# Attention and mixture-of-experts layer: a new order of work between the two stages, one PSUM place per tile for the last expert, and the variance's constant moved to VectorE

## The chip, the cores and the metric

One core of a Trainium2 chip. The metric is the device time of one execution in microseconds; lower is better. The kernel before takes 196.55 us (median of 3 runs, 196.53 to 196.87).

## The reference

The input is a tensor of 8 batches, 256 tokens each, 128 features. Two steps follow each other:

```
qkv = x @ w_qkv.T                 # 16 heads of 8 dimensions
att = softmax(mask(q k^T / sqrt(8)))    # keys i-127 .. i only
x   = layernorm(x + (att v) @ w_out.T)
probs = softmax(x @ router_w); top 2 of 8 experts per token, weights from probs
y   = sum over the 2 chosen experts of p * (gelu(x @ w_in[e] + b_in[e]) @ w_out[e] + b_out[e])
out = layernorm(x + y)            # (x - mean) / sqrt(var + 1e-5)
```

The kernel computes every expert for every token and multiplies with a gate that is zero where the expert wasn't chosen.

## The kernel before, in words

It is written engine by engine: each engine has its own list of instructions, in an order fixed by hand, and they meet through semaphores.

**Attention.** The batches 0 to 7 go through a pipeline of slots. A slot holds at most one pair of heads on each engine. For a pair n (8 per batch, 64 in all), PE multiplies keys by queries (`turned_scores`, L1067), ACT takes the exponential of the result into `probs` (L486), and for each two pairs (a quad, 4 per batch) POOL sets the forbidden places to zero with two affine selects (`mask_probs`, L443 and L445), whereupon PE weighs the values (`weigh_values`, L1089 and L1091) into `o_bank`. Up to pair 53 the scores go into the pair of PSUM banks `st`; pairs 54 and later alternate between `st` and `score_banks` 0 and 1, so that `turned_scores` of pair n waits only for exponential n - 2.

A batch is finished by a chain over four engines: ACT copies `o_bank` (`copy_output`, L528), PE transposes it (`turn_output`, L1127), VectorE divides by the sums (`normalise`, L735 and L743), PE transposes (`turn_attention`, L1138), ACT copies (L535), PE multiplies by the output weights (`project_out`, L1145), VectorE adds the residual and takes the statistics (L751, L758, L764), POOL takes variance plus constant to the power -1/2 (`first_deviation`, L435 and L437), VectorE normalises (`first_norm`, L770), PE transposes (`turn_x1`, L1154), ACT copies (L543), VectorE splits the copy into two halves of precision (L777, L779), and PE multiplies by the router's weights (L1161).

**Between the stages.** The slots 65 and later hold no new scores of a batch, only the last eleven pairs and what remains of batches 5, 6 and 7. There PE's slots are filled up with products of zeros that nobody reads (`keep_warm`, L977, two of 128x512 in each of eight slots). In the same slots VectorE splits the experts' first weights (`split_weights`, L784 and L786, 1024 columns each) and chooses the experts of the first four batches (`route_shift`, `choose`: L664 to L694, small operations of 64 columns in a row that depend on each other).

**Experts.** The tokens go in four chunks c of 512, a chunk in four tiles of 128. Per chunk and expert PE multiplies by the first weights in three passes (`first_layer`, L1173), ACT applies gelu (L594), PE multiplies by the second weights, four tiles into the four quarters of one PSUM bank (`second_layer`, L1187), and VectorE adds each tile, times its gate, to the rows (`add_share`, L860). After the last expert of a chunk VectorE takes statistics of the rows (`second_stats` L902, `second_moments` L908); POOL adds the constant (L468) and takes the power (L470), both for half a chunk, two tiles, at a time (`second_deviation`). In the last chunk VectorE normalises (`second_norm`, L915) and SP stores each half (L353).

```
second_layer(c, e):   wait gelu_done;  wait y_added >= (n - 3) * 4;  4 tiles;  y_ready += 1
add_last_expert(c):   wait y_ready;  shares 0, 1, 2;  stats of half 0;  share 3;
                      moments of half 0;  stats of half 1;  moments of half 1
```

Of the kernel before, what the change touches and what calls it, by code (L numbers as in the profile page):

```python
# [7 lines left out]
ALU = mybir.AluOpType  # L8
# [3 lines left out]
P = 128  # L12
B = 8
T = 256
E = 128
H = 16
D = E // H
NX = 8
# [8 lines left out]
QUADS = H // 4  # L27
TILES = B * T // P
CH = 512
CT = CH // P  # L30
NCH = B * T // CH
# [49 lines left out]
def attention_moe(nc, x_t, x, wqkv_t, wout_t, router_w, w_in, b_in_t, w_out, b_out, out):  # L81
    scratch = nc.dram_tensor("scratch", [2, 2, ROWS, 2, PAIRS * T], BF16, kind="Internal").ap()

    with ExitStack() as ctx:  # L84
# [3 lines left out]
        def sem(name):  # L88
            return ctx.enter_context(nc.semaphore(name))
# [7 lines left out]
        hid_bank = [score_bank[2], score_bank[0]]  # L97
        y_bank = [score_bank[1], st[:, 0, :], st[:, 1, :], o_bank[:, :]]
        gate_bank, bias_bank = misc

        ident = sb("ident", [P, P])
        ident_bf = sb("ident_bf", [P, P], BF16)
# [99 lines left out]
        hid_ready, gelu_done, y_ready, y_added = sem("hid_ready"), sem("gelu_done"), sem("y_ready"), sem("y_added")  # L202
        bias_added, stats2_done, moments2_done = sem("bias_added"), sem("stats2_done"), sem("moments2_done")
        eps2_added, rstd2_done, y_normed = sem("eps2_added"), sem("rstd2_done"), sem("y_normed")
        shift2_ready = sem("shift2_ready")
        stored = [sem(f"stored{i}") for i in range(2)]

        def pair_banks(n):
# [151 lines left out]
        def _(pool):  # L360
# [103 lines left out]
            def second_deviation(c):  # L464
                for half in range(2):
                    two = slice(2 * half, 2 * half + 2)
                    pool.wait_ge(moments2_done, c * CT + 2 * half + 2)
                    pool.tensor_scalar(var2[:, two], moments2[:, two, 1], EPS, None, ALU.add).then_inc(eps2_added, 1)  # L468
                    pool.wait_ge(eps2_added, c * 2 + half + 1)
                    pool.tensor_tensor(rstd2[:, two], var2[:, two], half_power[:, two], ALU.pow).then_inc(rstd2_done, 1)  # L470

# [7 lines left out]
        def _(act):  # L479
# [71 lines left out]
            def route_exponentials(tiles, k):  # L551

                act.wait_ge(route_shifted, k)
                nc.scalar.activation(route[1][:, tiles, :], route[0][:, tiles, :], ACT.Exp).then_inc(route_exp, 1)
# [18 lines left out]
            for n in range(PICKED):  # L573
                take_even(n)

            for slot in range(LAST_S2 + 1):
                n = pair_at(slot)
                if n is not None:
                    exponentials(*n)
                for offset, piece in ((TURN_MAX, copy_max), (TURN_ATTN, copy_attention), (PROJECT_QK, take_top), (PROJECT_QK + 1, take_middle),  # L580
                                      (VALUES, pad_v), (COPY_O, copy_output), (TURN_X1, copy_x1), (LOGITS, copy_logits)):
                    b = batch_at(slot, offset)
                    if b is not None:
                        piece(b)
                if slot == LAST_S1 + 3:
                    route_exponentials(EARLY, 1)

            def gelu(c, e):

# [57 lines left out]
        def _(dve):  # L647
# [208 lines left out]
            def token_rows(c, n):  # L856
                return x1[:, c * CT + n, :]

            def add_share(c, e, n):
                nc.vector.scalar_tensor_tensor(token_rows(c, n), y_bank[e % 4][:, n * E:(n + 1) * E], gate[:, c * CT + n, e:e + 1],  # L860
                                               token_rows(c, n), ALU.mult, ALU.add).then_inc(y_added, 1)

            def add_tile(c, e, n):
# [14 lines left out]
            def add_last_expert(c):  # L878

                dve.wait_ge(y_ready, c * NX + NX)  # L880
                for n in range(3):
                    dve.wait_ge(y_added, c * (NX * CT) + (NX - 2) * CT + n + 1)
                    add_share(c, NX - 1, n)
                second_stats(c, 0)
                dve.wait_ge(y_added, c * (NX * CT) + (NX - 1) * CT)
                add_share(c, NX - 1, 3)
                second_moments(c, 0)
                second_stats(c, 1)
                second_moments(c, 1)

            def add_bias(c):

                dve.wait_ge(bias_ready, c + 1)
                dve.wait_ge(y_added, c * (NX * CT) + (NX - 2) * CT)
                rows = x1[:, c * CT:(c + 1) * CT, :]
                nc.vector.tensor_tensor(rows, bias_bank[:, :].rearrange("p (n e) -> p n e", n=CT), rows, ALU.add).then_inc(bias_added, 1)
# [7 lines left out]
            def second_moments(c, half):  # L904

                dve.wait_ge(stats2_done, c * CT + 2 * half + 2)
                for n in (2 * half, 2 * half + 1):
                    nc.vector.bn_aggr(moments2[:, n, :], stats2[:, n, :]).then_inc(moments2_done, 1)  # L908

            def second_norm(c, half):  # L910

# [45 lines left out]
            for c in range(2, NCH):  # L957
                add_expert(c, 0)
                second_shift(c - 1)
                for e in range(1, NX - 2):  # L960
                    add_expert(c, e)
                add_bias(c)
                add_expert(c, NX - 2)
                dve.wait_ge(y_normed, c * CT)
                add_last_expert(c)
            second_norm(NCH - 1, 0)
            second_norm(NCH - 1, 1)

# [2 lines left out]
        def _(pe):  # L971
            mm = nc.tensor.matmul

            def keep_warm(count, bank=o_bank[:, :]):

                for _ in range(count):
                    mm(bank, idle_rows[:, 0:P], idle_rows[:, :], start=True, stop=True)  # L977
# [186 lines left out]
            def first_layer(c, e):  # L1164

                n = c * NX + e
                if n == 1:
                    pe.wait_ge(exp_done, B * PAIRS - 1)
                if n >= 2:
                    pe.wait_ge(gelu_done, n - 1)  # L1170
                cols = slice(c * CH, (c + 1) * CH)
                for i, (w, xx) in enumerate(((w_in_lo, x1_hi), (w_in_hi, x1_lo), (w_in_hi, x1_hi))):
                    last = mm(hid_bank[e % 2], w[:, e, :], xx[:, cols], start=i == 0, stop=i == 2)  # L1173
                last.then_inc(hid_ready, 1)

            def second_layer(c, e):

                n = c * NX + e
                pe.wait_ge(gelu_done, n + 1)
                if n >= 4:  # L1180
                    pe.wait_ge(y_added, (n - 3) * CT)
                if n == 1:
                    pe.wait_ge(exp_done, B * PAIRS)
                if n == 3:
                    pe.wait_ge(o_copied, B)
                for i in range(CT):
                    last = mm(y_bank[e % 4][:, i * E:(i + 1) * E], hid[e % 2][:, i * P:(i + 1) * P], w_out_sb[:, e, :], start=True, stop=True)  # L1187
                last.then_inc(y_ready, 1)

            def turn_gates(c):  # L1190

# [33 lines left out]
                pick_pair(n)  # L1225
            pe.wait_ge(consts_ready, 7)

            for slot in range(LAST_S2 + 1):
                n = pair_at(slot)
                if n is not None:  # L1230
                    turned_scores(*n)
# [45 lines left out]
                b = batch_at(slot, PROJECT_QK + 1)  # L1277
                if b is not None:
                    subtract_top(b)
                if slot > LAST_S1 + 1 and slot < LAST_S2 - 1:  # L1280
                    keep_warm(2, hid_bank[0])
                if slot == LAST_S2 - 1:
                    pe.wait_ge(w_lo_done, 1)
                    first_layer(0, 0)

            weigh_values(B - 1, QUADS - 2)
            first_layer(0, 1)
            second_layer(0, 0)
            weigh_values(B - 1, QUADS - 1)
            unit(0, 2)  # L1290
            turn_x1(B - 2)
            unit(0, 3)
# [71 lines left out]
```

## Time and profile before

| | |
|---|---|
| median of 3 runs | 196.55 us |
| the profiled execution, its own time | 196.5 us |
| its span, first to last instruction | 194.8 us |
| PE busy | 169.4 us (87%) |
| VectorE busy | 154.8 us (79%) |
| ACT busy | 114.6 us (59%) |
| POOL busy | 84.1 us (43%) |
| mean granted TensorE clock | 0.994 |

Times in the profile count from the start of the span; 1.7 us of the execution lie outside it. The attention pipeline with its eleven last pairs ends at about 128 us, the experts of chunk 0 begin there, chunk 3 ends at 188 us, and what follows is VectorE, POOL and the stores.

### The profile page before, as it was taken

To read this page: it belongs to the slowest core of one execution; us is meant where nothing else is said; L and a number is where in the kernel's file an instruction comes from. 1 tells how busy PE (TensorE), PEld (TensorE's weight loads), DVE (VectorE), ACT (ScalarE), POOL (GpSimd) and SP (SyncE) were. 2 spreads that over 40 slices of the span, in tenths; PEclk is the share of its full clock that TensorE was granted. 3 is DMA by queue.
4 is the path that set the end of the run, shared out by engine and by line. 5 is a ranking of instruction groups with operands and counts; after the bars stand their busy time and mean duration, and the time that the engine had idled before them with its cause. 6 is when DMAs were issued, how large, how long until landed. Compare 5 with 4: busy or idle time off the path is not lost. (4 is left out here: it accounts for less than half of the span.)

```text
span 194.8 us, 6184 instructions
## 1 busy us (share of the span) xinstructions
PE 169.4 (87%) x2450; PEld 121.5 (62%) x2460; DVE 154.8 (79%) x468; ACT 114.6 (59%) x216; POOL 84.1 (43%) x157
## 2 busy tenths in 40 slices
PE   7579887988989989889999899989999979999950
PEld 3354454655656656556656544558988869999950
DVE  6985959669598698697988999635798869898793
ACT  4542056687686766876857757564353784564720
POOL 7960006556563655746738366561043002603003
PEclk9999999999999999999999999999999999999997
DMA  5589594194780882955901000000000000020011
GB/s 142 148 232 222 168 242 132 53 212 125 158 226 11 176 206 72 214 160 110 218 13 57 2 8 0 3 0 0 5 0 0 3 27 27 0 59 0 3 53 54
DMA packets 23127, 17.25 MB, mean 89 GB/s; under 512 B 1827, under 2 KB 21179, under 8 KB 23099
## 3 DMA queue, kind: packets, MB, share of 16 engines
q1 hardware_dynamic: 23099, 16.87, 35.2%
q8 instruction: 19, 0.31, 0.7%
q14 instruction: 9, 0.07, 0.1%
HBM read 9.35 MB, written 7.34 MB: 86 GB/s over the span
## 5 line engine op out<-in xcount | busy, mean ns | idle before, releaser
L486 ACT ACTIVATE probs<-st 128x768 f32<-128x768 f32 x59 | 47.9, 811 | 23.8 <-PE st L1067 20.6
L443 POOL TENSOR_SCALAR_AFFINE_SELECT probs<-probs 128x1024 f32<-128x1024 f32 x32 | 35.1, 1097 | 57.4 <-ACT probs L486 57.3
L713 DVE TENSOR_REDUCE max_parts<-score_banks 128x2 f32<-128x384 f32 x64 | 32.6, 550 | 4.6 <-PE score_banks L1041 4.2
L594 ACT ACTIVATE hid<-score_banks,b_in_sb 128x512 f32<-128x512 f32 x32 | 21.9, 687 | 21.0 <-PE score_banks L1173 20.9
L716 DVE TENSOR_REDUCE max_parts<-score_banks 128x4 f32<-128x512 f32 x32 | 20.6, 686 | 13.6 <-PE score_banks L1041 13.6
L1067 PE MATMUL st<-stack 51*64 51x256 bf16 (+1 forms) x472 | 21.2, 254 | 6.2 <-ACT probs L486 5.7
L1030 PE MATMUL score_banks<-edges,ident_bf 64*64 64x256 bf16 (+1 forms) x192 | 19.0, 296 | 4.5 <-DVE max_parts L713 3.4
L1089 PE MATMUL o_bank<-probs,v 128*32 128x256 f32 x256 | 20.4, 391 | 0.0
L445 POOL TENSOR_SCALAR_AFFINE_SELECT probs<-probs 128x512 f32<-128x512 f32 x32 | 20.3, 634 | 0.0
L1067 PEld LDWEIGHTS st<-stack 51*64 51x64 bf16 (+1 forms) x472 | 8.6, 104 | 18.7 <-ACT probs L486 11.8
L860 DVE SCALAR_TENSOR_TENSOR x_rows<-st,gate,x_rows 128x128 f32<-128x128 f32 x64 | 18.1, 344 | 2.4 <-PE st L1187 2.0
L1041 PE MATMUL score_banks<-stack 48*64 48x192 bf16 (+2 forms) x512 | 19.1, 224 | 0.0
L1187 PEld LDWEIGHTS st<-w_out_sb,hid 128*128 128x128 f32 x128 | 16.6, 191 | 2.9 <-ACT hid L594 1.7
L1187 PE MATMUL st<-w_out_sb,hid 128*128 128x128 f32 x128 | 17.0, 276 | 1.3 <-ACT hid L594 1.3
L1173 PE MATMUL score_banks<-x_hi,w_in_lo 128*128 128x512 f32 x32 | 15.4, 480 | 0.0
L1030 PEld LDWEIGHTS score_banks<-edges,ident_bf 64*64 64x64 bf16 x192 | 7.5, 105 | 10.3 <-DVE max_parts L713 4.7
L1041 PEld LDWEIGHTS score_banks<-stack 48*64 48x64 bf16 x512 | 13.9, 107 | 0.0
L1091 PE MATMUL o_bank<-probs,v 128*32 128x128 f32 x256 | 12.9, 273 | 0.0
L1173 PE MATMUL score_banks<-x_hi,w_in_hi 128*128 128x512 f32 x32 | 12.6, 393 | 0.0
L1173 PE MATMUL score_banks<-x_lo,w_in_hi 128*128 128x512 f32 x32 | 12.6, 393 | 0.0
L468 POOL TENSOR_SCALAR var<-moments 128x2 f32<-128x2 f32 x8 | 1.7, 216 | 24.1 <-DVE moments L908 24.1
L1091 PEld LDWEIGHTS o_bank<-probs,v 128*32 128x32 f32 x256 | 8.3, 110 | 5.5
(136 smaller groups left out, 331.2 us busy)
## 6 DMA issues: line engine op xcount, KB each, us to landing
stack<-scratch SPq DMA_DIRECT2D x28, 192.0 KB, 4.0
scratch<-parts SPq DMA_DIRECT2D x16, 192.0 KB, 4.0
scratch<-parts SPq DMA_DIRECT2D x24, 128.0 KB, 3.8
x_rows<-x SPq DMA_DIRECT2D x4, 256.0 KB, 5.6
out<-y_sb SPq DMA_DIRECT2D x8, 128.0 KB, 1.8
x_t_sb<-x_t SPq DMA_DIRECT2D x3, 256.0 KB, 4.8
w_in_sb<-w_in SPq DMA_DIRECT2D x1, 512.0 KB, 5.8
w_out_sb<-w_out SPq DMA_DIRECT2D x1, 512.0 KB, 7.9
```

Of the source, the lines that this page charges most:

```text
L443: pool.affine_select(out=own, in_=own, compare_op=ALU.is_ge, fill=0.0, base=0, pattern=[[0, 2], [0, 4], [1, P]], channel_multiplier=-1).th ...
L486: nc.scalar.activation(probs[g][:, :, two, :].rearrange("p k j c -> p j k c"), pair_banks(PAIRS * b + p)[:, :, 0:3 * P].rearrange("p j (k ...
L594: nc.scalar.activation(hid[e % 2][:, :], hid_bank[e % 2], ACT.Gelu_apprx_tanh, bias=b_in_sb[:, e:e + 1]).then_inc(gelu_done, 1)
L713: nc.vector.tensor_reduce(top[:, 1, r, pair:pair + 2], bank[:, 0:384].rearrange("p (h c) -> p h c", h=2), X_AXIS, ALU.max, negate=True).th ...
L716: nc.vector.tensor_reduce(top[:, 0, r, pair:pair + 4], bank[:, :].rearrange("p (h c) -> p h c", h=4), X_AXIS, ALU.max, negate=True).then_i ...
L1030: mm(at, ident_bf[rows, 64 * r:64 * r + 64], mask, start=True, stop=True)
L1041: last = mm(bank[lo:lo + 64, i * width:i * width + keys.stop - keys.start], q[rows, pair + i, queries], k[rows, pair + i, keys], start=Fal ...
L1067: last = mm(to[cols, r, kt * T:kt * P + T], k[rows, p, at:at + 64], q[rows, p, kt * P:T], start=b > 0 or kt == 0, stop=b > 0, skip_group_c ...
L1089: last = mm(o_bank[rows, t * T:(t + 1) * T], v, probs[g][:, 0:2, j, :], start=s == 0, stop=s == 1, skip_group_check=True)
L1091: last = mm(o_bank[rows, t * T + P:(t + 1) * T], v, probs[g][:, 2, j, :], start=False, stop=s == 1, skip_group_check=True)
L1173: last = mm(hid_bank[e % 2], w[:, e, :], xx[:, cols], start=i == 0, stop=i == 2)
L1187: last = mm(y_bank[e % 4][:, i * E:(i + 1) * E], hid[e % 2][:, i * P:(i + 1) * P], w_out_sb[:, e, :], start=True, stop=True)
```

## The change

Three edits.

- PE and ACT leave the slot loop after slot 64, and what they do from there to the first layer of the first expert is written out in a list of its own. The 16 products of zeros become 2. On PE `weigh_values` comes before `turn_attention` of batch 5, pair 62 of the scores comes after `turn_attention` of batch 6 and not before, and the first layer of expert 0 comes after the last scores. On ACT `copy_output` of batch 6 comes two exponentials earlier, and the copy of batch 6's attention one. VectorE's, POOL's and SP's loops over the slots are as they were.
- In chunk 3 the second layer of expert 7 writes its four tiles into four different banks, with a signal after each; VectorE takes shares 0 and 1, statistics and moments of half 0, then the same for half 1. PE waits there for one more expert's shares (29 * 4 instead of 28 * 4).
- In all four chunks variance plus constant is computed on VectorE behind `bn_aggr`, and POOL is left with the power.

```diff
+        last_banks = [y_bank[(NX - 1) % 4][:, 0:E], gate_bank[:, 0:E], hid_bank[0][:, 0:E], y_bank[(NX - 4) % 4][:, 0:E]]
...
             def second_deviation(c):
                 for half in range(2):
                     two = slice(2 * half, 2 * half + 2)
-                    pool.wait_ge(moments2_done, c * CT + 2 * half + 2)
-                    pool.tensor_scalar(var2[:, two], moments2[:, two, 1], EPS, None, ALU.add).then_inc(eps2_added, 1)
                     pool.wait_ge(eps2_added, c * 2 + half + 1)
                     pool.tensor_tensor(rstd2[:, two], var2[:, two], half_power[:, two], ALU.pow).then_inc(rstd2_done, 1)
...
-            for slot in range(LAST_S2 + 1):
+            for slot in range(LAST_S1 + 1):
...
+            late, last = B - 2, B - 1
+            exponentials(late, 5)
+            copy_max(last)
+            exponentials(late, 6)
+            copy_attention(late - 1)
+            exponentials(late, 7)
+            route_exponentials(EARLY, 1)
+            exponentials(last, 0)
+            exponentials(last, 1)
+            pad_v(last)
+            copy_output(late)
+            exponentials(last, 2)
+            exponentials(last, 3)
+            copy_x1(late - 1)
+            exponentials(last, 4)
+            copy_logits(late - 1)
+            exponentials(last, 5)
+            copy_attention(late)
+            exponentials(last, 6)
+            exponentials(last, 7)
...
+            def finish_last_expert(c):
+
+                for half in range(2):
+                    for n in (2 * half, 2 * half + 1):
+                        dve.wait_ge(last_tiles, n + 1)
+                        dve.wait_ge(y_added, c * (NX * CT) + (NX - 2) * CT + n + 1)
+                        add_share(c, NX - 1, n)
+                    second_stats(c, half)
+                    second_moments(c, half)
...
                 for n in (2 * half, 2 * half + 1):
                     nc.vector.bn_aggr(moments2[:, n, :], stats2[:, n, :]).then_inc(moments2_done, 1)
+                two = slice(2 * half, 2 * half + 2)
+                dve.wait_ge(moments2_done, c * CT + 2 * half + 2)
+                if c:
+                    dve.wait_ge(rstd2_done, (c - 1) * 2 + half + 1)
+                nc.vector.tensor_scalar(var2[:, two], moments2[:, two, 1], EPS, None, ALU.add).then_inc(eps2_added, 1)
...
                 if n >= 4:
-                    pe.wait_ge(y_added, (n - 3) * CT)
+                    pe.wait_ge(y_added, (n - 3 + (n == NCH * NX - 1)) * CT)
...
-                if slot > LAST_S1 + 1 and slot < LAST_S2 - 1:
-                    keep_warm(2, hid_bank[0])
-                if slot == LAST_S2 - 1:
-                    pe.wait_ge(w_lo_done, 1)
-                    first_layer(0, 0)
-
-            weigh_values(B - 1, QUADS - 2)
+
+            late, last = B - 2, B - 1
+            turned_scores(late, 5)
+            turn_max(last)
+            turned_scores(late, 6)
+            weigh_values(late, 1)
+            turn_attention(late - 1)
+            turned_scores(late, 7)
+            weigh_values(late, 2)
+            project_out(late - 1)
+            keep_warm(2, hid_bank[0])
+            turned_scores(last, 0)
+            turned_scores(last, 1)
+            project_v(last)
+            weigh_values(late, 3)
+            turned_scores(last, 2)
+            turned_scores(last, 3)
+            turn_x1(late - 1)
+            turn_output(late)
+            turned_scores(last, 4)
+            route_logits(late - 1)
+            weigh_values(last, 0)
+            turned_scores(last, 5)
+            turn_attention(late)
+            turned_scores(last, 6)
+            weigh_values(last, 1)
+            project_out(late)
+            turned_scores(last, 7)
+            weigh_values(last, 2)
+            pe.wait_ge(w_lo_done, 1)
+            first_layer(0, 0)
             first_layer(0, 1)
             second_layer(0, 0)
-            weigh_values(B - 1, QUADS - 1)
+            weigh_values(last, 3)
```

PE at the start of the stretch between the stages, before: pair 54 of the scores (L1067), `turn_attention` of batch 5 (L1138), `weigh_values` (L1089, L1091), products of zeros (L977), pair 55, `project_out` (L1145).

```order
L1067 MATMUL score_banks<-stack 64x256 x4
L1067 MATMUL score_banks<-stack 64x128 x4
L1138 MATMUL misc<-ident,attn 128x128 x2
L1089 MATMUL o_bank<-probs,v 32x256 x4
L1091 MATMUL o_bank<-probs,v 32x128 x4
L977 MATMUL score_banks<-idle_rows 128x512 x2
L1067 MATMUL st<-stack 64x256 x4
L1067 MATMUL st<-stack 64x128 x4
L1145 MATMUL misc<-wout_sb,attn_t 128x128 x2
```

The same place in the changed kernel, whose line numbers are 38 higher here.

```order
L1105 MATMUL score_banks<-stack 64x256 x4
L1105 MATMUL score_banks<-stack 64x128 x4
L1127 MATMUL o_bank<-probs,v 32x256 x4
L1129 MATMUL o_bank<-probs,v 32x128 x4
L1176 MATMUL misc<-ident,attn 128x128 x2
L1105 MATMUL st<-stack 64x256 x4
L1105 MATMUL st<-stack 64x128 x4
L1127 MATMUL o_bank<-probs,v 32x256 x4
L1129 MATMUL o_bank<-probs,v 32x128 x4
L1183 MATMUL misc<-wout_sb,attn_t 128x128 x2
```

`weigh_values` has moved ahead of the transposition, and pair 55 follows that directly, with neither `weigh_values` nor products of zeros between them.

VectorE at the end of the program, before: the shares of expert 7 (L860), statistics (L902), moments (L908), normalisation (L915).

```order
L860 SCALAR_TENSOR_TENSOR x_rows<-o_bank,gate,x_rows 128x128 x3
L902 BN_STATS stats<-x_rows 128x6 x2
L860 SCALAR_TENSOR_TENSOR x_rows<-o_bank,gate,x_rows 128x128
L908 BN_AGGR moments<-stats 128x2 x2
L902 BN_STATS stats<-x_rows 128x6 x2
L908 BN_AGGR moments<-stats 128x2 x2
L915 TENSOR_SCALAR y_sb<-x_rows,moments,rstd 128x128 x4
```

The same place in the changed kernel (L943 is variance plus constant).

```order
L880 SCALAR_TENSOR_TENSOR x_rows<-o_bank,gate,x_rows 128x128
L880 SCALAR_TENSOR_TENSOR x_rows<-misc,gate,x_rows 128x128
L932 BN_STATS stats<-x_rows 128x6 x2
L938 BN_AGGR moments<-stats 128x2 x2
L943 TENSOR_SCALAR var<-moments 128x2
L880 SCALAR_TENSOR_TENSOR x_rows<-score_banks,gate,x_rows 128x128 x2
L932 BN_STATS stats<-x_rows 128x6 x2
L938 BN_AGGR moments<-stats 128x2 x2
L943 TENSOR_SCALAR var<-moments 128x2
L950 TENSOR_SCALAR y_sb<-x_rows,moments,rstd 128x128 x4
```

Every operation of half 0 now directly follows the one that it needs, and two operations are added.

## Rows read from the trace of the kernel before

**Rows 1.** Busy us by stretch: PE, PE's weight loads, VectorE, ACT, POOL; then granted clock.
```profile
112.00:125.00 13.00, 12.10 (x161) 6.14 (x164) 12.14 (x34) 8.11 (x18) 7.66 (x10) 1.00 0.01 3
157.40:187.80 30.40, 30.40 (x223) 27.99 (x223) 25.78 (x103) 17.77 (x32) 5.94 (x16) 1.00 0.08 23
```
**Rows 2.** The chain of waits, in order of time: start us, us, what.
```profile
187.91 1.03 DVE x_rows L860 x4
...
189.83 0.22 POOL var L468
...
191.07 0.75 POOLq L84
```
**Rows 3.** Timeline of VectorE between the stages: start us, us, operation, [idle before].
```profile
114.20 1.22 DVE L786 TENSOR_TENSOR w_in_lo<-w_in_sb,w_in_hi 128x1024 fp32r<-128x1024 f32 x1
...
117.48 0.23 DVE L675 TENSOR_TENSOR route<-route,row_stat 128x64 f32<-128x64 f32 x1
...
118.26 1.07 DVE L678 TENSOR_TENSOR route<-route,row_stat 128x64 f32<-128x64 f32 x1
...
121.37 0.93 DVE L678 TENSOR_TENSOR route<-route,row_stat 128x64 f32<-128x64 f32 x1
...
124.25 0.62 DVE L743 TENSOR_TENSOR attn<-misc,inv_sum 128x64 f32<-128x64 f32 x4
128.14 0.43 DVE L751 TENSOR_TENSOR resid<-misc,x_rows 128x256 f32<-128x256 f32 x1 [3.27 <-PE misc L1145]
```
**Rows 4.** Timeline of POOL between the stages.
```profile
115.18 1.20 POOL L443 TENSOR_SCALAR_AFFINE_SELECT probs<-probs 128x1024 f32<-128x1024 f32 x1 [1.56 <-ACT probs L486]
...
117.23 0.70 POOL L437 TENSOR_TENSOR rstd<-var_eps,half_power 128x2 f32<-128x2 f32 x1
118.16 1.09 POOL L443 TENSOR_SCALAR_AFFINE_SELECT probs<-probs 128x1024 f32<-128x1024 f32 x1 [0.23 <-ACT probs L486]
```
**Rows 5.** Timeline of PE between the stages.
```profile
112.20 0.44 PE L1138 MATMUL misc<-ident,attn 128*128 128x128 f32 x2 [0.68 <-ACT max_t L508]
...
115.54 0.64 PE L1089 MATMUL o_bank<-probs,v 128*32 128x256 f32 x8
...
116.33 0.60 PE L977 MATMUL score_banks<-idle_rows 128*128 128x512 bf16 x2
...
120.23 0.44 PE L1154 MATMUL misc<-ident,x_rows 128*128 128x128 f32 x2
...
125.05 0.44 PE L1138 MATMUL misc<-ident,attn 128*128 128x128 f32 x2
...
130.38 1.16 PE L1187 MATMUL score_banks<-w_out_sb,hid 128*128 128x128 f32 x8 [0.60 <-ACT hid L594]
```
**Rows 6.** Timeline of ACT: exponential 55, the last of batch 6.
```profile
114.30 0.81 ACT L486 ACTIVATE probs<-st 128x768 f32<-128x768 f32 x1 [1.18 <-PE st L1067]
```
**Rows 7.** Timeline of VectorE at the end.
```profile
187.04 1.13 DVE L860 SCALAR_TENSOR_TENSOR x_rows<-st,gate,x_rows 128x128 f32<-128x128 f32 x4
188.09 0.86 DVE L860 SCALAR_TENSOR_TENSOR x_rows<-o_bank,gate,x_rows 128x128 f32<-128x128 f32 x3
188.86 0.48 DVE L902 BATCH_NORM_STATS2 stats<-x_rows 128x6 f32<-128x128 f32 x2
...
189.50 0.24 DVE L908 BATCH_NORM_AGGREGATE moments<-stats 128x2 f32<-128x6 f32 x2
189.66 0.46 DVE L902 BATCH_NORM_STATS2 stats<-x_rows 128x6 f32<-128x128 f32 x2
190.15 0.25 DVE L908 BATCH_NORM_AGGREGATE moments<-stats 128x2 f32<-128x6 f32 x2
```
**Rows 8.** Timeline of VectorE behind chunk 0: the smallest operation, and its wait.
```profile
150.36 0.16 DVE L921 SCALAR_TENSOR_TENSOR shift<-moments,rstd 128x4 f32<-128x4 f32 x1 [0.47 <-POOL rstd L470]
```
**Rows 9.** The two stretches behind PE's last product; third number from the right: granted clock.
```profile
187.90:192.40 4.50, 0.00 (x0) 0.00 (x0) 3.62 (x18) 0.00 (x0) 1.81 (x4) 1.00 0.10 30
192.40:194.80 2.40, 0.00 (x0) 0.00 (x0) 0.05 (x1) 0.00 (x0) 0.00 (x0) 0.51 0.37 108
```

More of the change, by code:

```diff
@@ L204, in attention_moe @@
         eps2_added, rstd2_done, y_normed = sem("eps2_added"), sem("rstd2_done"), sem("y_normed")
-        shift2_ready = sem("shift2_ready")
+        shift2_ready, last_tiles = sem("shift2_ready"), sem("last_tiles")
         stored = [sem(f"stored{i}") for i in range(2)]
@@ L584, in _ @@
                         piece(b)
-                if slot == LAST_S1 + 3:
-                    route_exponentials(EARLY, 1)
+            late, last = B - 2, B - 1
[18 more added lines that the diff above has]
+            exponentials(last, 7)
             def gelu(c, e):
@@ L859, in add_share @@
             def add_share(c, e, n):
-                nc.vector.scalar_tensor_tensor(token_rows(c, n), y_bank[e % 4][:, n * E:(n + 1) * E], gate[:, c * CT + n, e:e + 1],
+                y = last_banks[n] if c * NX + e == NCH * NX - 1 else y_bank[e % 4][:, n * E:(n + 1) * E]
+                nc.vector.scalar_tensor_tensor(token_rows(c, n), y, gate[:, c * CT + n, e:e + 1],
                                                token_rows(c, n), ALU.mult, ALU.add).then_inc(y_added, 1)
@@ L964, in _ @@
                 dve.wait_ge(y_normed, c * CT)
-                add_last_expert(c)
+                if c < NCH - 1:
+                    add_last_expert(c)
+                else:
+                    finish_last_expert(c)
             second_norm(NCH - 1, 0)
@@ L1186, in second_layer @@
                 for i in range(CT):
-                    last = mm(y_bank[e % 4][:, i * E:(i + 1) * E], hid[e % 2][:, i * P:(i + 1) * P], w_out_sb[:, e, :], start=True, stop=True)
-                last.then_inc(y_ready, 1)
+                    at = y_bank[e % 4][:, i * E:(i + 1) * E]
+                    if n == NCH * NX - 1:
+                        at = last_banks[i]
+                    last = mm(at, hid[e % 2][:, i * P:(i + 1) * P], w_out_sb[:, e, :], start=True, stop=True)
+                    if n == NCH * NX - 1:
+                        last.then_inc(last_tiles, 1)
+                if n < NCH * NX - 1:
+                    last.then_inc(y_ready, 1)
             def turn_gates(c):
@@ L1226, in _ @@
             pe.wait_ge(consts_ready, 7)
-            for slot in range(LAST_S2 + 1):
+            for slot in range(LAST_S1 + 1):
                 n = pair_at(slot)
```

## The prediction

> **What bounds the kernel now.** I read the busy times by stretch first, then the chain of waits, then the timelines of the engines at the two places that the change touches.
>
> From 157.4 to 187.8 us PE is busy without a gap, 30.40 of 30.40 us [rows 1]. Its work there is untouched, so whatever time PE loses or wins before it arrives at the end undiminished. Between the stages, from 112 to 125 us, two engines are nearly full: PE with 12.10 us, part of which is products of zeros, and VectorE with 12.14 us, all of it needed [rows 1]. The difference matters. The filler on PE can only be won if nobody else sets the pace. The timeline says who does: `normalise` of batch 6 starts at 124.25 and ends at 124.87 [rows 3], and PE transposes its result at 125.05, 0.18 us later [rows 5]. VectorE has no such partner: it waits for PE only behind that, 3.27 us at 128.14 [rows 3]. So between the stages **VectorE is the bound**, and PE's filler stands in time that PE would otherwise wait.
>
> At the end the chain is VectorE's shares (from 187.91), then POOL's four operations, the last of them done at 191.82 [rows 2]. PE isn't in it: its last product ends at 187.9, while VectorE takes up expert 7 at 188.09 directly behind expert 6, four shares at a distance of 0.26 us from 187.04 [rows 7].
>
> **Part 1: the new order between the stages.** It removes 14 products of zeros. Two of them take 0.60 us [rows 5], so some 4 us of PE, at nothing or at a gain of nothing as long as VectorE is the cover. What moves VectorE? Its list is the same; only POOL can disturb it.
>
> Step a, when POOL comes. `turn_attention` of batch 5 can't start before 112.20 in either kernel: it waits for ACT's copy, and PE stood idle 0.68 us for it [rows 5]. The `weigh_values` that is now put into that idle time takes 0.79 us (115.54 to 116.33, [rows 5]), so the transposition starts at about 112.24. The scores of pair 55 follow it directly; before, `weigh_values` (0.79) and two products of zeros (about 0.54 net of overlap) stood between. So exponential 55, at 114.30 before [rows 6], comes 1.3 us earlier, at 113.0, and POOL's mask, at 115.18 before [rows 4], comes at about 113.9.
>
> Step b, what it meets. VectorE's split of the experts' weights (L786) begins at 114.20 and takes 1.22 us [rows 3]; before, POOL was idle then. It reads two operands from SBUF. What such an operation does when it meets a mask, the rows show: the same small operation of 128x64 took 1.07 us at 118.26 and 0.93 us at 121.37, where its neighbour took 0.23 [rows 3], and the first ended at 119.33, 0.08 us behind POOL's mask of 118.16 to 119.25 [rows 4]. So VectorE stands until the mask ends. The new mask's first part lasts from 113.9 to 115.0 (1.09, [rows 4]); L786 then ends at about 116.1 to 116.2 and not at 115.42: **+0.7 us**. If POOL's second part (0.64 us) slips in first it is +1.3; if exponential 55 comes 0.3 us later than I think, L786 is first and it is 0.
>
> Step c, the other meetings. Before, the small operations lost 0.84 us at 118.26 and 0.70 at 121.37 (above 0.23), and less at two others. Shifted by 0.7 they meet masks that now begin at about 118.3 (behind exponential 57 and POOL's deviation of batch 5) and 120.2 (behind exponential 59). Going through the list I find again three meetings, at the fourth small operation (0.8), at the second half of `first_norm` (0 to 0.9) and at the first operation of the second choice (0.6). That is 0.3 us less or 0.5 more than before. `normalise` of batch 6 then ends at 125.2 to 125.6, not at 124.87: **+0.35 to +0.7 us, I take +0.45**, since most settings of the small offsets give values near the lower end.
>
> Step d, what hangs on it. Behind `turn_attention` of batch 6 PE has about the same time to go to the last scores in both orders: before `weigh_values`, a first layer, then the scores; now the scores of pair 62, `weigh_values`, `project_out`, and then the scores, both about 2 us. Behind the last exponential come the table load for gelu, gelu, and the second layer of expert 0 at 130.38, for which PE waits 0.60 us [rows 5]. So this also moves by +0.45, and the rest of PE behind it. `project_out` of batch 6 comes about 0.6 us earlier, into VectorE's idle 3.27 us: worth nothing, since POOL's deviation follows the last mask.
>
> **Part 2: the constant on VectorE.** In chunks 0 to 2 it adds two operations per chunk, with the wait in front of each about 0.2 us, so 0.4 us. It takes away the constant's 0.3 us on POOL, and VectorE then waits less for the power: 0.47 us before [rows 8]. I count it as 0; if the cover were gone (no wait there), it would be 0.4 us of VectorE per chunk, in a stretch where PE has no gap. The Trainium skill, page "SBUF — State Buffer", section "Who interferes with whom", says that a VectorE operation with two SBUF inputs fully blocks while POOL reads SBUF. For the masks the trace agrees. For POOL's power it doesn't: it ran from 117.23 for 0.70 us [rows 4], and VectorE's operation with two SBUF inputs at 117.48 took its 0.23 us [rows 3]. I go by the row; by the rule a part of each power would be added here, at most 0.7 us per chunk.
>
> **Part 3: the end.** Starting from the share at 188.09, the old order reaches its last moments at 190.15 [rows 7]: it puts share 2 between share 1 and the statistics, and share 3 between statistics and moments, so no operation waits for the one directly ahead. In the new order each one does. A share followed by another takes 0.26 us, by something that needs it 0.37 (its duration 0.34, as three take 0.86, plus the 0.03 between 190.12 and 190.15). Two statistics with the moments behind them take 0.51 (0.48 + 0.03), later 0.49; two moments 0.16 until the next operation, 0.28 until one that needs them. The new list: 0.26 + 0.37 + 0.51 + 0.28, the constant 0.10 until the next share, 0.26 + 0.37 + 0.49 = 2.64 us, so the last moments start at 190.73. Then 0.28, the constant 0.16 (the nearest row is 128x4 with 0.16, [rows 8]), 0.09 to POOL, the power 0.70, 0.04 back: normalisation at 192.00. Before, it follows the power that ended at 191.82 [rows 2]; with 0.03 that is 191.85. So **+0.15 us**; between +0.05, if the constant takes half as long, and +0.3, if the gap behind a share is 0.10 instead of 0.03. The tiles' own signals and banks bring nothing, as VectorE is busy with expert 6 until 188.09; PE's longer wait costs nothing: the shares of expert 4, for which it now also waits, are added two experts before those of 187.04. Taking POOL's two constants away (0.21 and a 0.09 gap each, [rows 2] for one) would bring 0.45 us under the old order; the new order spends it.
>
> **Sum.** 0.45 + 0 + 0.15 = +0.6 us on the profiled execution's 196.5 us, which gives 197.1. The median is 196.55, so it stands the same.
>
> **The rivals.**
>
> *The masks miss.* POOL's mask comes after 114.20, VectorE isn't touched, and `normalise` ends as before. For it: the margin is 0.3 us, made of several 0.05 us latencies. Against it: each has its row. The time is 196.5 + 0 + 0.15 = 196.65, with other meetings 196.4 to 196.9. Chance 0.20.
>
> *Faster: VectorE's collisions thin out.* Its 12.9 us between 112 and 125 hold about 3 us of standing behind masks. If the earlier masks fall on reductions and PSUM reads, which the rows don't show to be delayed, `normalise` ends before 124.4, and PE, without filler, is ready for it. With 1 us won and the end as costed it is 195.7; it decides from 0.6 us won upwards. Chance 0.14.
>
> *The end wins.* If the pipeline of VectorE carries dependent operations better than my gaps, the end gains up to 0.4 us instead of losing 0.15, and the sum is 196.5. Chance 0.10. The rows on dependent pairs speak against it.
>
> *The clock falls.* Without filler PE stands from about 118.4 (scores of pair 59) until batch 5 is normalised (120.23 before, [rows 5]; 120.8 to 121.9 now). That is 2.4 to 3.5 us. The granted clock stayed at 2.4 GHz for 4.5 us without a product at the end, then fell to 1.2 [rows 9], which speaks against a fall. If it fell, the 2.5 us of PE's work behind it would double, partly inside PE's wait for `normalise`: 198 to 199.5. Chance 0.04. The Trainium skill, "TensorE: Matmul & The Clock Gate", "HAM oscillation — how this bites in real kernels", warns of such gaps, which speaks against removing the filler.
>
> **The numbers.** My own case has 0.52, with 196.8 to 197.7 as its own range. A measurement of this kernel can tell about 0.2% (0.4 us), so faster means below 196.16, slower above 196.94. Slower: 0.52 less 0.03 at its lower edge, clock 0.04, edges of others 0.05 = 0.58. Same: misses 0.17, end 0.08, edge 0.03 = 0.28. Faster: 0.14. The range reaches from 196.0 to 197.9; outside lie most of the faster case and the clock.
>
> **What would show it.** Exponential 55 near 113.0; L786 at 1.9 us; `normalise` of batch 6 ending near 125.3; a wait of PE of over 2 us before `turn_x1` of batch 5; the first second layer near 130.8; at the end 3.9 us, not 3.76, from the first share of expert 7 to the last normalisation. Wrong: L786 at 1.22 us, or `turn_attention` of batch 6 before 124.9.

## The result, and the profile after

| | before | changed |
|---|---|---|
| median, us | 196.56 (4 runs, 196.53 to 196.87) | 200.44 (4 runs, 199.98 to 200.57) |
| ratio | 1 | 1.0189, 95% interval 1.017 to 1.0209 |
| profiled execution: time, span, mean clock | 196.5, 194.8, 0.994 | 200.34, 198.6, 0.968 |

The change costs 3.9 us. The forecast was 197.1 us with a range to 197.9: the side is right, the size is not. In some executions all work comes about 0.5 us or 0.6 us later, from the first exponential on (27.6 to 27.8 us instead of 27.1) and so long ahead of what the change touches; of the traces below those of e2, e5, e8, e10 and e11 are such.

One line of the page shows most of it: the granted clock in 40 slices of 5 us, in tenths. Before there was a 9 everywhere until the last slice.

```profile
PEclk9999999999999999999999997579999999999997
```

The dip lies between the stages. Busy us by stretch of the changed kernel (PE, PE's weight loads, VectorE, ACT, POOL, then granted clock); the last row is the stretch of experts, which answers to [rows 1]:

```profile
112.00:118.60 6.60, 5.36 (x96) 1.00 0.02 6
```
```profile
118.00:120.00 2.00, 0.60 (x24) 0.31 (x16) 1.83 (x5) 1.84 (x4) 2.00 (x3) 1.00 0.00 0
120.00:122.00 2.00, 0.00 (x0) 0.00 (x0) 1.96 (x4) 0.22 (x1) 1.89 (x3) 0.79 0.00 0
122.00:124.00 2.00, 1.90 (x14) 1.33 (x14) 1.75 (x9) 0.38 (x1) 0.00 (x0) 0.50 0.00 0
124.00:130.00 6.00, 6.00 (x63) 3.37 (x57) 1.62 (x8) 2.89 (x5) 1.68 (x2) 0.50 0.01 3
130.00:132.00 2.00, 2.00 (x28) 0.99 (x27) 1.16 (x5) 0.83 (x2) 0.00 (x0) 0.65 0.00 0
...
160.90:191.40 30.50, 30.44 (x223) 28.06 (x223) 26.28 (x107) 17.91 (x33) 5.06 (x12) 1.00 0.08 23
```

(The first row is PE's alone.) PE was busy for 5.36 of the 6.60 us before 118.60, then did nothing. A mean of 0.79 over 120 to 122 is full clock (2.4 GHz) for 1.2 us and half (1.2 GHz) behind it, so it fell near 121.2, **2.6 us after PE's last product ended**; 0.65 over 130 to 132 puts its return near 131.4. It was low for 10.2 us. From 122.1 to 131.4, over 9 us, PE works in it without a gap.

PE's timeline of the changed kernel, to be laid beside [rows 5]:

```profile
118.27 0.34 PE L1105 MATMUL st<-stack 51*64 51x256 bf16 x8
122.10 0.69 PE L1192 MATMUL misc<-ident,x_rows 128*128 128x128 f32 x2 [3.50 <-DVE x_rows L789]
...
124.99 1.08 PE L1127 MATMUL o_bank<-probs,v 128*32 128x256 f32 x8
```
```profile
134.01 1.16 PE L1228 MATMUL score_banks<-w_out_sb,hid 128*128 128x128 f32 x8 [0.38 <-ACT hid L613]
```

`turn_x1` waits 3.50 us for VectorE and then takes 0.69 us, not 0.44; eight products of `weigh_values` take 1.08, not 0.64. The second layer of expert 0 begins at 134.01, where before it began at 130.38: +3.63 us, and the first share of expert 7 at the end comes +3.63 us later as well (191.72 for 188.09).

VectorE, beside [rows 3], and POOL, beside [rows 4]:

```profile
114.27 2.00 DVE L805 TENSOR_TENSOR w_in_lo<-w_in_sb,w_in_hi 128x1024 fp32r<-128x1024 f32 x1
...
118.55 1.15 DVE L695 TENSOR_TENSOR route<-route,rank_w 128x64 f32<-128x64 f32 x1
...
120.32 1.73 DVE L789 TENSOR_SCALAR x_rows<-resid,moments,rstd 128x128 f32<-128x128 f32 x2
...
125.09 0.62 DVE L762 TENSOR_TENSOR attn<-misc,inv_sum 128x64 f32<-128x64 f32 x4
```
```profile
113.96 1.23 POOL L445 TENSOR_SCALAR_AFFINE_SELECT probs<-probs 128x1024 f32<-128x1024 f32 x1 [0.27 <-ACT probs L486]
115.14 1.62 POOL L447 TENSOR_SCALAR_AFFINE_SELECT probs<-probs 128x512 f32<-128x512 f32 x1
...
118.53 1.09 POOL L445 TENSOR_SCALAR_AFFINE_SELECT probs<-probs 128x1024 f32<-128x1024 f32 x1
...
120.28 1.10 POOL L445 TENSOR_SCALAR_AFFINE_SELECT probs<-probs 128x1024 f32<-128x1024 f32 x1
121.33 0.64 POOL L447 TENSOR_SCALAR_AFFINE_SELECT probs<-probs 128x512 f32<-128x512 f32 x1
```

The split of the weights meets the mask that came early and takes 2.00 us, where it took 1.22. `normalise` of batch 6 ends at 125.71, not 124.87: +0.84.

The end, beside [rows 7], on VectorE and POOL:

```profile
191.72 0.34 DVE L880 SCALAR_TENSOR_TENSOR x_rows<-o_bank,gate,x_rows 128x128 f32<-128x128 f32 x1
...
193.16 0.17 DVE L943 TENSOR_SCALAR var<-moments 128x2 f32<-128x2 f32 x1
...
194.93 0.73 POOL L470 TENSOR_TENSOR rstd<-var,half_power 128x2 f32<-128x2 f32 x1 [0.83 <-DVE var L943]
195.69 0.60 DVE L950 TENSOR_SCALAR y_sb<-x_rows,moments,rstd 128x128 f32<-128x128 f32 x2 [0.33 <-POOL rstd L470]
```

From the first share of expert 7 to the last normalisation 3.97 us pass, 3.76 before: +0.21. With the 3.63 us this is 3.84, the whole difference of the two profiled executions. The views don't say how the 3.63 us divide between the half clock and VectorE's later work, since the two lie in the same stretch. That needs the runs.

### The profile page after: what moved, and what is told of

The parts are those of the page before. It is cut to its first block, busy times and chain, and to the rows that moved or that the text cites. A ratio compares the mean times of both kernels' runs of the same rounds, so it can differ in the third digit from the quotient of the medians.

```text
span 198.6 us, 6175 instructions
## 1 busy us (share of the span) xinstructions
PE 171.6 (86%) x2446; PEld 122.9 (62%) x2446; DVE 156.9 (79%) x476; ACT 114.4 (58%) x216; POOL 83.6 (42%) x149
## 4 chain that ended last, share of the span: by engine, by line
PE 60%; DVE 21%; ACT 10%; issue 5%; DMA 1%; POOLq 0%; SPq 0%; POOL 0%; DVEq 0%; ACTq 0%
PE score_banks L1211 10%; PE st L1228 7%; PE st L1105 6%; PE o_bank L1127 5%; ACT probs L486 5%; DVE max_parts L735 4%; PE misc L1021 4%; DVE x_rows L789 3%; PE o_bank L1015 3%; DVE max_parts L732 3%; PE score_banks L1068 3%; PE score_banks L1079 3%; PE score_banks L1228 3%; PE o_bank L1228 3%; PE misc L1183 2%
## 5 line engine op out<-in xcount | busy, mean ns | idle before, releaser
L735 DVE TENSOR_REDUCE max_parts<-score_banks 128x4 f32<-128x512 f32 x32 | 20.6, 686 | 13.7 <-PE score_banks L1079 13.6
L1127 PE MATMUL o_bank<-probs,v 128*32 128x256 f32 x256 | 21.5, 409 | 0.7 <-POOL probs L447 0.7
L447 POOL TENSOR_SCALAR_AFFINE_SELECT probs<-probs 128x512 f32<-128x512 f32 x32 | 21.4, 667 | 0.0
L470 POOL TENSOR_TENSOR rstd<-var,half_power 128x2 f32<-128x2 f32 x8 | 5.6, 697 | 26.2 <-DVE var L943 26.2
L1129 PE MATMUL o_bank<-probs,v 128*32 128x128 f32 x256 | 13.4, 282 | 0.0
```

Of the source, the lines that this page charges most:

```text
L735: nc.vector.tensor_reduce(top[:, 0, r, pair:pair + 4], bank[:, :].rearrange("p (h c) -> p h c", h=4), X_AXIS, ALU.max, negate=True).then_i ...
L1127: last = mm(o_bank[rows, t * T:(t + 1) * T], v, probs[g][:, 0:2, j, :], start=s == 0, stop=s == 1, skip_group_check=True)
L1129: last = mm(o_bank[rows, t * T + P:(t + 1) * T], v, probs[g][:, 2, j, :], start=False, stop=s == 1, skip_group_check=True)
```

## The experiments

My first theory: the clock costs some 2.8 us, VectorE's collisions with masks 0.8, the end 0.2. The rival: the new order costs about 3.6 us by itself, through its waits, and the clock is only a sign of it. Each run's ratio is to the kernel before, run beside it on the same chip (median 196.76 us for the first four, 196.55 for the next four, 196.52 for the last three). None of the edits leaves out anything whose result is read.

### e1: the changed kernel with products of zeros where PE stops

```diff
             turned_scores(last, 3)
+            keep_warm(12, hid_bank[0])
             turn_x1(late - 1)
```

> The changed kernel with 12 products of zeros (some 2.6 us of PE) put in front of turn_x1 of batch 5, where PE stood idle for 3.50 us. Theory 1 (the clock): the granted clock fell to 1.2 GHz in that idle time and this costs most of the 3.9 us; the filler keeps it at 2.4 GHz, normalise of batch 6 still ends 0.8 us later than before, the end still takes 0.2 us more: 197.6 us, clock 0.99 or more. Theory 2 (the order itself): scores of pair 62 behind turn_attention and VectorE's lateness make the whole loss, the clock is only a symptom: 200 us or more. If the filler delays turn_x1, its own time shows as well.

197.6 us (12 runs), ratio 1.0047 [1.0033, 1.0061]: 2.8 us of the 3.9 are gone, by adding work to PE. PE and the clock of this run:

```profile
118.72 2.54 PE L1015 MATMUL score_banks<-idle_rows 128*128 128x512 bf16 x11 [0.16 <-issue]
122.06 0.44 PE L1192 MATMUL misc<-ident,x_rows 128*128 128x128 f32 x2 [0.80 <-DVE x_rows L789]
...
125.81 0.41 PE L1176 MATMUL misc<-ident,attn 128*128 128x128 f32 x2 [0.97 <-DVE attn L762]
...
131.14 1.16 PE L1228 MATMUL score_banks<-w_out_sb,hid 128*128 128x128 f32 x8 [0.55 <-ACT hid L613]
```
```profile
122.00:124.00 2.00, 1.94 (x26) 1.53 (x30) 1.73 (x10) 1.05 (x2) 0.00 (x0) 1.00 0.00 0
```

`turn_x1` starts at the same moment as in the changed kernel (122.06 for 122.10), since VectorE sets it, but from there to the second layer 9.08 us pass instead of 11.91. That is the clock's price, 2.83 us, with the same order. The rest is what the prediction was made of: the second layer 0.76 us later than before, and the end 3.98 us long. The rival falls: with VectorE as late as in the changed kernel, 2.8 us are gone once the clock stays up.

### e2, e3 and e4: the parts alone

e2 is the kernel before with the end by halves and the constant on VectorE, and the old order between the stages:

```diff
+            def finish_last_expert(c):
...
-                    pool.tensor_scalar(var2[:, two], moments2[:, two, 1], EPS, None, ALU.add).then_inc(eps2_added, 1)
...
+                nc.vector.tensor_scalar(var2[:, two], moments2[:, two, 1], EPS, None, ALU.add).then_inc(eps2_added, 1)
```

> The kernel before with the last expert's tiles by halves and the constant on VectorE, without the new order between the stages. Theory 1: 196.55 + 0.2 = 196.75 us, the last normalisation 3.95 us behind the first share of expert 7 (3.76 before). Theory 2 says the same. If the end were a gain as its three edits intend: 196.1 us.

196.94 us, ratio 1.0005 [0.9991, 1.0019]; the end takes 3.97 us as in the changed kernel. The time can't be told from no change; the timeline's +0.21 us fits in the interval.

e3 has the last two of those lines alone, and keeps the old order of the shares.

> The kernel before with only the constant moved to VectorE, shares and statistics in the old order. If dependent neighbours cost what I counted: half 1's moments end at 190.40, constant 0.17, power 0.70, so the last normalisation comes 0.45 us earlier: 196.1 us. If VectorE's two more operations per chunk weigh in chunks 0 to 2 (0.4 us each, no cover): up to 197.3 us.

196.79 us, ratio 0.9989 [0.9974, 1.0005]: 0.7 us above the expected 196.1, and not to be told from no change. VectorE and POOL at the end of e3:

```profile
189.58 0.24 DVE L906 BATCH_NORM_AGGREGATE moments<-stats 128x2 f32<-128x6 f32 x2
189.86 0.17 DVE L911 TENSOR_SCALAR var<-moments 128x2 f32<-128x2 f32 x1
...
190.11 0.69 POOL L468 TENSOR_TENSOR rstd<-var,half_power 128x2 f32<-128x2 f32 x1 [11.24 <-DVE var L911]
190.45 0.25 DVE L906 BATCH_NORM_AGGREGATE moments<-stats 128x2 f32<-128x6 f32 x2
190.73 0.17 DVE L911 TENSOR_SCALAR var<-moments 128x2 f32<-128x2 f32 x1
...
190.98 0.74 POOL L468 TENSOR_TENSOR rstd<-var,half_power 128x2 f32<-128x2 f32 x1 [0.18 <-DVE var L911]
191.76 0.60 DVE L918 TENSOR_SCALAR y_sb<-x_rows,moments,rstd 128x128 f32<-128x128 f32 x2 [0.32 <-POOL rstd L468]
```

From the share at 188.16 to the last normalisation 3.60 us pass, 0.16 less than before and not 0.45. The constant has not gone, it has changed its engine: VectorE waits for its own moments (0.28 us from 189.58 to 189.86), and the second moments, behind the first constant, start 2.29 us after the share and not 2.06. What POOL no longer does VectorE does earlier in the chain. The 0.16 us fit in the interval.

e4 is the new order alone, with the old end.

> The kernel before with only the new order between the stages. Theory 1 and theory 2: the changed kernel's time less 0.2 us, so 200.2 us, with the clock at 1.2 GHz for some 10 us after 121. If the loss came from the two parts together: near 196.6 or near 200.4.

200.05 us (6 runs, 199.12 to 200.89), ratio 1.0161 [1.0137, 1.0186]: the order carries nearly all of the loss. In the profiled execution (199.12 us) the stop before `turn_x1` is again 3.50 us, and the clock falls a little later:

```profile
120.00:122.00 2.00, 0.00 (x0) 0.00 (x0) 1.96 (x4) 0.19 (x1) 1.87 (x3) 1.00 0.00 0
122.00:124.00 2.00, 1.92 (x22) 1.59 (x22) 1.73 (x10) 1.03 (x2) 0.00 (x0) 0.84 0.00 0
```
```profile
130.00:130.50 0.50, 0.50 (x12) 0.81 0.00 0
```

A mean of 0.84 over 122 to 124 puts the fall near 123.4: here it came when PE was already at work again. The second row, PE's alone, puts the return near 130.2. So the clock was low for 6.8 us and not for 10.2, and from `turn_x1` (122.08) to the second layer (133.00) 10.92 us pass instead of 11.91. That is 1.0 of the 1.2 us by which this execution is faster than the changed kernel's; the old end is the rest. The moment of the fall isn't fixed by the instructions alone, and the price goes with how long the clock stays low. The 1.8 us between the lowest and the highest of the six times may be that; only one of them has a trace.

### e5: is it the one long stop?

My second theory was that the long stop does it, and that the fillers between short ones don't matter. e5 keeps the old order and takes out its products of zeros:

```diff
-                if slot > LAST_S1 + 1 and slot < LAST_S2 - 1:
-                    keep_warm(2, hid_bank[0])
```

> The kernel before, its order kept, with all 16 products of zeros between the stages left out. If filler as such keeps the clock: PE's waits get longer everywhere, the clock falls, 199 us or more. Theory 1 (the fall needs one long stop of PE, which the new order and VectorE's lateness make together): exponential 55 comes 0.5 us earlier, its mask after VectorE's 114.20, so the weight split isn't met; PE's stop before turn_x1 stays under 3 us, the clock stays at 2.4 GHz, 196.3 to 197.3 us.

198.56 us, ratio 1.0096 [1.0078, 1.0115]: a miss, and the theory with it. PE and the clock of e5:

```profile
121.45 0.44 PE L1154 MATMUL misc<-ident,x_rows 128*128 128x128 f32 x2 [2.16 <-DVE x_rows L770]
```
```profile
118.00:120.00 2.00, 1.29 (x32) 0.56 (x25) 1.83 (x6) 1.97 (x7) 2.00 (x3) 1.00 0.00 0
120.00:122.00 2.00, 0.55 (x10) 0.35 (x10) 1.98 (x3) 0.72 (x3) 1.90 (x3) 1.00 0.00 0
122.00:124.00 2.00, 2.00 (x24) 1.64 (x20) 1.75 (x8) 1.28 (x3) 0.00 (x0) 0.65 0.00 0
```

With a stop of 2.16 us the clock fell as well, near 122.6, and was low until 129.4, for 6.8 us. VectorE is not what this run loses: its `normalise` ends at 125.51 in a trace whose stretch lies 0.66 us late (the split's first half starts at 113.69 instead of 113.03), which is 124.85, as before. The second layer of expert 0, at 132.61, comes 1.6 us later than before, the 0.66 taken off. **The products of zeros of the kernel before are load-bearing**: without them it loses 2.0 us on the median, in its own order, and 1.6 of them are seen in this stretch of the profiled execution. That is what the forecast left out where it put 14 of them "at nothing".

### e6, e7 and e8: the split of the weights moved out of the mask's way

`split_weights` goes behind `normalise` of batch 6. e6 does it in the changed kernel, e7 in the kernel before with the constant on VectorE, e8 in the new order with the constant and the old end.

```diff
-                if slot == LAST_S1 + 2:
-                    split_weights()
...
                     normalise(b)
+                if slot == LAST_S1 + 9:
+                    split_weights()
```

> The changed kernel with split_weights on VectorE moved from behind route_shift to behind normalise of batch 6, into the time in which VectorE was idle. Theory 1: the mask no longer meets the weight split, VectorE's chain to first_norm of batch 5 is 3 us shorter, PE's stop before turn_x1 goes from 3.5 us to under 1 us without any filler, the clock stays at 2.4 GHz; normalise of batch 6 ends at 122.5 to 123.7; with the end's 0.2 us 195.0 to 196.0 us. Theory 2 (the order of PE makes the loss): still 199 us or more.

> The kernel before with the same move of split_weights, and the constant on VectorE in the old order of the end. VectorE is then no longer the bound between the stages, but PE with its filler is: it had only 0.2 us of waiting left there. 196.2 to 196.5 us. If VectorE was the only bound: 195.3 us.

> The new order between the stages, split_weights late, the constant on VectorE, the old order of the end: what I think is left of the change when the collision and the dependent end are taken away. 0.3 to 0.4 us under e6_after_late_split: 194.7 to 195.6 us.

All three miss: 198.61 (1.0104 [1.007, 1.0139]), 197.6 (1.0049 [1.003, 1.0068]) and 198.06 us (1.0058 [1.0037, 1.0079]). In e6 and e8 PE's stop shrinks to 1.80 us, and the clock still falls; e6:

```profile
119.76 0.44 PE L1192 MATMUL misc<-ident,x_rows 128*128 128x128 f32 x2 [1.80 <-DVE x_rows L789]
```
```profile
120.00:122.00 2.00, 2.00 (x18) 1.39 (x16) 1.88 (x4) 0.92 (x2) 1.65 (x2) 0.56 0.00 0
```
```profile
133.50:134.00 0.50, 0.50 (x5) 0.59 0.00 0
```

In e6 it fell near 120.2, half a microsecond after PE had begun again, and by the second row, PE's alone, came back near 133.9: 13.7 us, in the slowest of its four executions (199.59 us). In e8 it fell near 122.2, 2.0 us after PE had begun again, and was low for 6.8 us. VectorE also gained less than expected: in e6 `normalise` ends at 124.48, 0.4 us earlier than in the kernel before and not at 122.5 to 123.7, since its small operations now meet other masks (0.74, 1.01 and 0.55 us instead of 0.23).

e7 keeps its fillers and its clock, but the split, now at 125.35, meets a later mask, and here PE waits for it:

```profile
125.35 2.07 DVE L784 TENSOR_TENSOR w_in_lo<-w_in_sb,w_in_hi 128x1024 fp32r<-128x1024 f32 x1
```
```profile
127.47 0.51 PE L1176 MATMUL score_banks<-x_hi,w_in_lo 128*128 128x512 f32 x1 [1.17 <-DVE w_in_lo L784]
```

The split was moved to where its reader is close behind it. In the old place PE needs it only much later.

### e9: four products instead of twelve

As e1, with `keep_warm(4, hid_bank[0])`.

> The changed kernel with 4 products of zeros (0.9 us) instead of 12 in front of turn_x1 of batch 5, which leaves some 2.6 us without a product. If only a stop of nearly 3.5 us brings the clock down, this is as fast as with 12: 197.6 us. If the clock goes by how little PE does over the whole stretch, as e5 and e6 (stops of 1.8 and 2.2 us, clock down) suggest, it falls here too, at least in some executions: 198.5 to 200.5 us.

Four executions, in two groups: 197.42 and 197.49 us with a mean clock of 0.992 and 0.993, 199.22 and 199.34 with 0.970 and 0.972. One program, and by the mean clock it falls in half of the executions; the first group has e1's time, the second is 1.8 us slower. The profiled execution is of the first group:

```profile
122.10 0.44 PE L1192 MATMUL misc<-ident,x_rows 128*128 128x128 f32 x2 [2.53 <-DVE x_rows L789]
```
```profile
120.00:122.00 2.00, 0.00 (x0) 0.00 (x0) 1.96 (x4) 0.22 (x1) 1.89 (x3) 1.00 0.00 0
```

So the clock held through a stop of 2.53 us here, where e6 lost it at one of 1.80. The length of the stop alone doesn't tell.

### e10 and e11: the choice of the experts moved, and a faster kernel

The second theory on VectorE: what delays it are the small operations of `choose`, which nobody needs soon and which stand ahead of `first_norm` of batch 5 and `normalise` of batch 6. Both kernels put them behind `normalise` of batch 6, and have the constant on VectorE and the old end. e10 has the new order with 8 products of zeros before `turn_x1`, e11 the old order with its own fillers.

```diff
-                if slot > LAST_S1 + 3 and slot <= LAST_S1 + 7:
-                    choose(EARLY, 1, slot - LAST_S1 - 4)
...
+                if slot == LAST_S1 + 9:
+                    choose(EARLY, 1, 0)
+                    choose(EARLY, 1, 1)
+                if slot > LAST_S1 + 9:
+                    choose(EARLY, 1, slot - LAST_S1 - 8)
```

> The new order on PE and ACT, the constant on VectorE with the old order of the end, 8 products of zeros before turn_x1 of batch 5, and on VectorE the choice of experts (16 small operations, 4.2 us) behind normalise of batch 6 and not before it. If VectorE was what bound the stretch and the fillers keep the clock: normalise of batch 6 ends at 122.8 instead of 125.71, the first second layer at 128.3, and the time is 194.3 to 195.0 us. If the clock falls all the same: 197 us or more.

> The kernel before, its order and its 16 products of zeros kept, with the same late choice of experts and the constant on VectorE. If PE with its fillers bounds as soon as VectorE doesn't: only the 0.2 us of waiting and the end's 0.1 go, 196.2 to 196.5 us; VectorE's relief is then worth something only together with the new order.

e10: **195.48 us** (4 runs), ratio 0.9942 [0.992, 0.9965], faster than both kernels, though 0.5 us above what I expected. e11: 196.63 us, ratio 1.0003 [0.9984, 1.0021]. Timelines of e10 (its whole stretch lies 0.6 us later than in the trace of the kernel before, as `split_weights` at 113.69 for 113.03 shows):

```profile
114.86 1.99 DVE L803 TENSOR_TENSOR w_in_lo<-w_in_sb,w_in_hi 128x1024 fp32r<-128x1024 f32 x1
...
123.19 0.61 DVE L760 TENSOR_TENSOR attn<-misc,inv_sum 128x64 f32<-128x64 f32 x4
```
```profile
119.35 1.67 PE L1002 MATMUL score_banks<-idle_rows 128*128 128x512 bf16 x7 [0.16 <-issue]
120.86 0.43 PE L1179 MATMUL misc<-ident,x_rows 128*128 128x128 f32 x2
...
129.28 1.16 PE L1212 MATMUL score_banks<-w_out_sb,hid 128*128 128x128 f32 x8 [0.53 <-ACT hid L611]
```

`normalise` ends at 123.80, over 1 us before the kernel before although all starts later, the clock stays up, and the second layer comes 1.10 us earlier. The split still meets its mask (1.99 us); what it would bring to avoid that isn't measured. In the old order (e11) the same VectorE list wins nothing, since PE with its 16 products sets the pace. VectorE is idle for 2 us there while PE is busy for 1.90, and `normalise` ends at 124.68, but PE comes to the transposition only at 125.64, without having waited for it (this trace too lies 0.6 us late).

```profile
120.00:122.00 2.00, 1.90 (x22) 0.67 (x22) 0.00 (x0) 1.26 (x3) 0.72 (x2) 1.00 0.00 0
```
```profile
124.06 0.62 DVE L741 TENSOR_TENSOR attn<-misc,inv_sum 128x64 f32<-128x64 f32 x4
```
```profile
125.64 0.44 PE L1144 MATMUL misc<-ident,attn 128*128 128x128 f32 x2
```

The new order won only in e10, with a shorter list ahead of `normalise` and with a filler in PE's stop. With the filler alone it didn't (e1). That e10 needs its filler is likely after e6 and e8, which lost the clock at a stop of 1.80 us, but no run has e10 without it.

## Why the prediction was wrong

**The step that failed** is the term for the removed products in part 1, "at nothing or at a gain of nothing as long as VectorE is the cover", with the argument that let it stand: "The granted clock stayed at 2.4 GHz for 4.5 us without a product at the end, then fell to 1.2 [rows 9], which speaks against a fall", and for the fall a chance of 0.04. What the runs show in its place is a clock at 1.2 GHz for 10.2 us and a price of 2.83 us (e1). The chance was drawn from one place of the trace, behind 30 us in which PE had been full [rows 1]; whether that fullness made the difference isn't shown. The place that the change makes is another one: behind 118.60 the clock held for 2.6 us. e5, e6 and e8 lost it with stops of 2.16, 1.80 and 1.80 us, and e9 in two executions of four. The case should have had most of the chance. The rule of the Trainium skill that the forecast named beside it ("TensorE: Matmul & The Clock Gate", "HAM oscillation — how this bites in real kernels") was the better guide. It warns of idle gaps of TensorE, and e1 agrees: with most of the 3.50 us filled the clock stays up. The falls in e5, e6 and e8, at stops of 2.16 us and less, go beyond what that section describes.

Its price was short as well. I let the clock double the "2.5 us of PE's work behind it" and came to 198 to 199.5. The low clock lasted 10.2 us, and PE was busy in all but the first 0.9 of them, and it cost 2.83; only waits as short as e1's 0.97 us before `turn_attention` and 0.55 before the second layer were there to take some of it up. e1's 197.6 and 2.8 make the 200.4 that was measured.

The other steps:
- Step a, exponential 55 at 113.0 and the mask at 113.9: 113.07 and 113.96. Right.
- Step b, "+0.7" for the split: 2.00 us instead of 1.22, +0.78. Right, and with it "the masks miss" is out.
- Step c, "+0.35 to +0.7 us, I take +0.45": +0.84 in the changed kernel, about +0.8 in e1, above even its upper end. Two of the three meetings named came: a small operation took 1.15 us, and `first_norm` 1.73, both its halves hit (0.81 before, so +0.9, the upper end of the step's "0 to 0.9" for its second half). The third, at the first operation of the second choice, didn't: 0.21 us. I took the lower end without a row that preferred it. Mis-sized by 0.4.
- Step d, that this carries to the second layer: +0.76 in e1, where the clock doesn't disturb it. Right.
- Part 2, the constant in chunks 0 to 2 at nothing: the stretch of experts moved by 3.63 us at both ends, and nothing was added in between. Right.
- Part 3, "+0.15": +0.21 in the changed kernel and in e2. Right. Its last sentence, that taking POOL's constants away would bring 0.45 us under the old order, is wrong: 0.16 (e3), as VectorE then waits for its own moments.
- "Faster: VectorE's collisions thin out" and "The end wins" didn't happen.
- The signs came for the most part: exponential 55, L786 at 2.00 us, PE's wait of 3.50, an end of 3.97; `normalise` was 0.4 us later than the sign and the second layer 3.2. None of the signs was the clock.

The sum corrected: 0.8 for VectorE, 0.2 for the end, 2.8 for the clock, 3.8 to 3.9 us in all; e1 has the first two alone and stands at 197.6.

## What to carry to other kernels

Products of zeros that stand in an engine's idle time are not free to remove: cost their removal by the work that follows at half the clock (it was low for 6.8 to 13.7 us in the five traces where it fell), and try the kernel with a filler in the new gap before judging an order. A trace that shows the clock holding through one stop doesn't show that it holds through another one, elsewhere in the program. An operation that is moved between engines or slots pays where its reader or its rival for SBUF stands next; look for both in the new place.

## What was not expected of the hardware

- The clock fell 2.6 us after the last product (121.2 in the changed kernel), and near 123.4 in e4 with the same 3.50 us stop, after PE had taken up its work again, as in e5, e6 and e8; it held for 4.5 us at the end [rows 9]. In e9 it fell in two of four executions. What decides between them stays open.
- At 1.2 GHz the products didn't all double: the eight of `weigh_values` went from 0.64 to 1.08 us, the transposition from 0.44 to 0.69.
- A delay by the meeting of VectorE and POOL goes both ways. POOL's second select took 1.62 us beside the end of the split, where elsewhere it takes 0.63 or 0.64; in e5, where VectorE came first, the first select took 1.73 instead of 1.09.
- Two operations of VectorE in a row can each stand behind one select of POOL's: `first_norm`'s halves took 1.73 us together, as long as the selects of 120.28 and 121.33 beside them (1.10 and 0.64).
